# The last four steps of a decoder-layer kernel: first-layer chunks of batch 14 among the last transposed scores, and the last batch's second layer, norm and store by halves of the tokens

## What is computed

```python
x = _layernorm(x + _L0_attn_ref(x, w_qkv, w_proj, q_norm_w, k_norm_w))
x = _layernorm(x + _L0_xattn_ref(x, ctx, ctx, mask, Wq, Wk, Wv, Wo))
x = _layernorm(x + _L0_ffn_ref(x, ...))      # light_out + heavy_out
# feedforward: h = rmsnorm(x, gamma); h = gelu(h @ w1.T + b1); h @ w2.T + b2
```

## Time and profile before

| | us |
|---|---|
| median of 3 runs | 975.88 (974.96 to 978.18) |
| profiled execution, its own time | 978.16 |
| its span, first to last instruction | 976.40 |
| PE busy over the span | 888.3 (91%) |
| DVE busy | 725.3 (74%) |
| POOL busy | 537.9 (55%) |
| ACT busy | 496.8 (51%) |
| mean granted PE clock | 0.960 of 2.4 GHz |

### The profile page before, as it was taken

How to read it: one execution, slowest core, us unless ns; L and a number is a source line. 1 busy time by engine, 2 the same in 40 slices (tenths; PEclk the granted TensorE clock), 3 DMA queues, 4 the chain that set the end, 5 groups by cost and what they waited for, 6 DMA issues and landing times. The chain is left out here.

```text
span 976.4 us, 21698 instructions
## 1 busy us (share of the span) xinstructions
PE 888.3 (91%) x7712; PEld 689.7 (71%) x7712; DVE 725.3 (74%) x1764; ACT 496.8 (51%) x1063; POOL 537.9 (55%) x1047
## 2 busy tenths in 40 slices
PE   3367897999999999999999999999999999999886
PEld 2335565787868787777878787877778686767576
DVE  7788687878788878879787888788887877663411
ACT  1132444646475655656464756556464746455332
POOL 7554465646564756656565647657565656162421
PEclk9669898999999999999999999999999999999888
DMA  3794383727476654818275666738283656613000
GB/s 110 120 173 68 52 110 50 106 33 109 51 100 78 98 78 65 111 37 110 34 119 59 100 78 80 97 54 107 44 109 42 95 72 88 77 31 49 14 11 21
DMA packets 79644, 74.22 MB, mean 76 GB/s; under 512 B 8593, under 2 KB 78897, under 8 KB 79537
## 3 DMA queue, kind: packets, MB, share of 16 engines
q1 hardware_dynamic: 75008, 68.11, 50.5%
q10 hardware_dynamic: 4528, 4.73, 1.9%
HBM read 17.49 MB, written 4.20 MB: 22 GB/s over the span
## 5 line engine op out<-in xcount | busy, mean ns | idle before, releaser
L768 ACT ACTIVATE pr<-bank 128x384 f32<-128x384 f32 x512 | 240.0, 500 | 188.1 <-PE bank L370 187.0
L946 DVE TENSOR_REDUCE mx<-bank 128x3 f32<-128x384 f32 x512 | 266.4, 552 | 89.7 <-PE bank L370 87.5
L1311 POOL TENSOR_SCALAR_AFFINE_SELECT pr<-pr 128x256 f32<-128x256 f32 x512 | 222.1, 448 | 132.3 <-ACT pr L768 130.1
L370 PE MATMUL bank<-w,g 128*128 128x256 f32 x576 | 170.8, 389 | 1.1 <-ACT g L780 1.1
L370 PE MATMUL bank<-cmaskb,idb 128*128 128x256 bf16 x512 | 143.3, 280 | 27.7 <-DMA stk2k<-nat1k 13.7
L780 ACT ACTIVATE g<-bank,b 128x256 f32<-128x256 f32 x144 | 67.8, 473 | 83.5 <-PE bank L370 83.2
L1335 POOL TENSOR_TENSOR xTlow<-xT,xThigh 128x512 fp32r<-128x512 f32 x16 | 20.8, 1301 | 149.8 <-ACT xThigh L702 149.8
L370 PEld LDWEIGHTS bank<-w,g 128*128 128x128 f32 x576 | 89.6, 190 | 5.2 <-ACT g L780 1.5
L370 PEld LDWEIGHTS bank<-cmaskb,idb 128*128 128x128 bf16 x512 | 50.1, 98 | 50.5 <-DVE mx L946 22.5
L370 PE MATMUL bank<-stk2k,stk2q 97*128 97x128 bf16 (+1 forms) x512 | 85.1, 253 | 0.0
L370 PE MATMUL bank<-stk1q,stk1k 100*128 100x256 bf16 (+1 forms) x512 | 80.1, 254 | 2.4 <-DMA stk1q<-mT 1.0
(11 more groups left out here) (166 smaller groups left out, 1832.5 us busy)
## 6 DMA issues: line engine op xcount, KB each, us to landing
stk1q<-nat1q SPq DMA_DIRECT2D x90, 128.0 KB, 4.5
stk1k<-nat1k SPq DMA_DIRECT2D x90, 128.0 KB, 5.4
stk2k<-nat2k SPq DMA_DIRECT2D x90, 128.0 KB, 4.6
stk2q<-nat2q SPq DMA_DIRECT2D x90, 128.0 KB, 5.7
xT<-in_xT SPq DMA_DIRECT2D x16, 256.0 KB, 5.9
ctxT<-in_ctxT SPq DMA_DIRECT2D x16, 256.0 KB, 6.0
x<-in_x SPq DMA_DIRECT2D x16, 256.0 KB, 5.7
out_x<-x SPq DMA_DIRECT2D x16, 256.0 KB, 2.2
```

Source lines behind the costliest of these rows:

```text
L370: return nc.tensor.matmul(out, lhsT, rhs, start=start, stop=stop, skip_group_check=check)
L768: nc.scalar.activation(pr[:, h % (2 * HG), :], ring_bank("T", a, b, h)[:, 0:3 * P], ACT.Exp, scale=HD ** -0.5)\
L946: V.tensor_reduce(mx3[:, h, :], scored[:, 0:3 * P].rearrange("p (k t) -> p k t", k=3), AX.X, ALU.max, negate=True).then_inc(s_mx[a], 1)
L1311: G.affine_select(out=slot, in_=slot, compare_op=ALU.is_ge, fill=0.0, base=0, pattern=[[0, 2], [1, P]], channel_multiplier=-1).then_inc(s_ ...
```

## The change

Only steps 15 to 19 differ.

- Step 15: the second half of batch 12's second layer (`FFN1`) moves from phase 3 to phase 4 (`FFN1_LATE`). Its residual and statistics on DVE move behind the norm of batch 15, its inverse deviation on POOL behind the last mask. The inverse deviation of batch 15 moves from head 13 to head 10.
- Step 16: four chunks of batch 13 stay in phase 1, five move to between the cross scores of phase 2; its first half's second layer moves to later heads. ACT loads GELU's table with a one-element GELU ahead of the step's work. Eight chunks of batch 14 move from step 17 to phase 4 of step 16, among the transposed cross scores of batch 15; each has half a bank of its own (banks 5, 6, 7, 4), so none waits for a GELU.
- Step 17: only chunk 8 of batch 14 stays. The eight other GELUs run on ACT after the last exponential; the copy for batch 15's output projection stands after seven of them (`COPY2_LAST`). The cross output of batch 15 uses banks 0, 1, 2 and 0. The transposes of its normalised tokens move from behind head 12 to head 3 of phase 3, so that they stand behind 12 of the 18 second-layer products of batch 14. The exponential's table is not loaded any more.
- Step 18: `last_ffn` runs the last batch's first layer in four banks, with the second layer of the first token half four chunks behind it, then the second half. Each half has a bank, a residual, statistics, inverse deviation, norm (on DVE) and store of its own.

```diff
+        def token_bank(b, t):
+            return bank[t if b == B - 1 else TOK_BANK[t]]
...
+        def hidden_out(b, j):
+
+            if b == B - 2 and j < LIGHT:
+                return bank[(5, 6, 7, 4)[j // 2]][:, j % 2 * T:(j % 2 + 1) * T]
+            if b == B - 2:
+                return bank[OT_BANK][:, T:2 * T]
+            return bank[(1, 2, 5, 6)[j % 4] if b == B - 1 else HIDDEN_BANK[j % 2]][:, 0:T]
...
-                if live(i - 4):
+                if i - 4 == B - 1:
+                    for t in range(TT):
+                        sp.wait_ge(s_x[3], TT * (B - 1) + t + 1)
+                        load(io["out"][B - 1, t * P:(t + 1) * P, :], xo[3][:, t, :], s_out)
+                elif live(i - 4):
...
                 if live(b + 1):
                     pe.wait_ge(s_mT[2], b + 2)
+                else:
+                    pe.wait_ge(s_g, FCH * (B - 2) + 6)
                 four_transposes(XNT_BANK, xn).then_inc(s_xnt, 1)
...
-                if j == 0:
+                if b == B - 1:
+                    if j == 0:
+                        pe.wait_ge(s_xnT, B)
+                        pe.wait_ge(s_on[2], TT * B)
+                    elif j == 1:
+                        pe.wait_ge(s_onT[2], B)
+                    elif j < 4:
+                        pe.wait_ge(s_g, FCH * (B - 2) + 2 * j - 2)
+                    else:
+                        pe.wait_ge(s_g, FCH * b + j - 3)
+                elif b == B - 2:
+                    if j == 0:
+                        pe.wait_ge(s_xnT, b + 1)
+                        pe.wait_ge(s_va[2], B)
+                    elif j == 2:
+                        pe.wait_ge(s_rest[2], 2 * B)
+                    elif j == 4:
+                        pe.wait_ge(s_mT[2], B)
+                    elif j == 6:
+                        pe.wait_ge(s_y[3], b)
+                    elif j == LIGHT:
+                        pe.wait_ge(s_oT[2], NG * B)
+                elif j == 0:
...
+            def last_ffn_out(t, j):
+
+                b = B - 1
+                pe.wait_ge(s_g, FCH * b + j + 1)
+                if t == 1 and j == 0:
+                    pe.wait_ge(s_y[2], B)
+                last = mm(bank[(3, 0)[t]][:, 0:D], g[:, j, t * P:(t + 1) * P], w2[:, j, :], j == 0, j == FCH - 1)
+                if j == FCH - 1:
+                    last.then_inc(s_o[3], 1)
+
+            def last_ffn():
+
+                for j in range(FCH + 4):
+                    if j >= 4:
+                        last_ffn_out(0, j - 4)
+                    if j < FCH:
+                        hidden(B - 1, j)
+                for j in range(FCH):
+                    last_ffn_out(1, j)
...
+                if l == B - 1:
+                    return last_ffn()
...
-                if live(l):
-                    for j in range(FCH):
+                if l == B - 2:
+                    add(6, hidden, l, LIGHT)
+                elif live(l):
+                    for j in range(FCH if l < B - 3 else HIDDEN_AHEAD):
                         add(HIDDEN_AT[j], hidden, l, j)
...
+                if l == B - 3:
+                    for j in range(HIDDEN_AHEAD, FCH):
+                        add(HIDDEN_BEHIND[j - HIDDEN_AHEAD], hidden, l, j)
                 if live(l):
                     for j in range(FCH):
-                        add(FFN0_AT[j], ffn_out, l, 0, j)
+                        add((FFN0_LATE if l == B - 3 else FFN0_AT)[j], ffn_out, l, 0, j)
...
-                    add(XNT_AT, transpose_xn, f)
-                if live(l):
+                    add(XNT_LAST if f == B - 1 else XNT_AT, transpose_xn, f)
+                if live(l) and l != B - 4:
...
+                if l == B - 4:
+                    for j in range(FCH):
+                        add(FFN1_LATE[j], ffn_out, l, 1, j)
+                if f == B - 2:
+                    for j in range(LIGHT):
+                        add(HIDDEN_LATE[j], hidden, f, j)
...
+                if c == B - 1:
+                    nc.scalar.activation(warmg[:, :], minus_half[:, 0:1], ACT.Gelu)
                 if live(c):
                     high_part(2, c, 0, 1)
                 for j in range(FCH):
-                    if j == COPY2_AT and live(f):
+                    if j == (COPY2_LAST if f == B - 1 else COPY2_AT) and live(f):
                         copy_out(f)
-                    if j == MIDQ_AT and live(c):
+                    if j == (0 if c == B - 1 else MIDQ_AT) and live(c):
                         mid_part(2, c, 0, 1)
...
-                wait(act, s_warm, i + 2)
-                nc.scalar.activation(warm[:, :], minus_half[:, 0:1], ACT.Exp).then_inc(s_warm, 1)
+                if i <= B:
+                    wait(act, s_warm, i + 2)
+                    nc.scalar.activation(warm[:, :], minus_half[:, 0:1], ACT.Exp).then_inc(s_warm, 1)
...
+            def last_tokens(t):
...
+                V.tensor_tensor(y[3][:, t, :], bank[(3, 0)[t]][:, 0:D], x2b[:, t, :], ALU.add).then_inc(s_ylast, 1)
...
+                V.bn_stats(st[3][:, t, :], y[3][:, t, :]).then_inc(s_bn[3], 1)
...
+                V.bn_aggr(mv[3][:, t, :], st[3][:, t, :]).then_inc(s_mv[3], 1)
+                dve.wait_ge(s_rslast, t + 1)
...
+                V.tensor_scalar(xo[3][:, t, :], y[3][:, t, :], mv[3][:, t, 0:1], rstd[3][:, t:t + 1],
+                                ALU.subtract, ALU.mult).then_inc(s_x[3], 1)
...
+                if l == B - 1:
+                    last_tokens(0)
+                    last_tokens(1)
+                elif live(l) and l != B - 4:
+                    residual_ffn()
...
                 if live(s):
                     layer_norm(1, s)
+                if l == B - 4:
+                    residual_ffn()
...
+                if l == B - 1:
+                    last_deviation(0)
+                    last_deviation(1)
                 roots = {}
-                if live(l):
+                if live(l) and l != B - 4 and l != B - 1:
                     roots[RSTD3_AT] = lambda: inverse_deviation(3, l)
                 if live(s):
-                    roots[RSTD1_AT] = lambda: inverse_deviation(1, s)
+                    roots[RSTD1_LAST if s == B - 1 else RSTD1_AT] = lambda: inverse_deviation(1, s)
...
+                if l == B - 4:
+                    inverse_deviation(3, l)
...
-MAX2_AT, XNT_AT = 5, 12
+MAX2_AT, XNT_AT, XNT_LAST = 5, 12, 3
+HIDDEN_AHEAD, HIDDEN_BEHIND = 4, (1, 2, 4, 5, 7)
+FFN0_LATE = (8, 9, 10, 11, 12, 13, 14, 15, 16)
+FFN1_LATE = (2, 4, 5, 6, 8, 10, 11, 12, 14)
+HIDDEN_LATE = (3, 4, 5, 6, 8, 9, 10, 12)
+COPY2_LAST = 7
...
-RSTD3_AT, RSTD1_AT = 3, 13
+RSTD3_AT, RSTD1_AT, RSTD1_LAST = 3, 13, 10
```

More of the change, by code:

```diff
@@ L250, in values_of, with dim_bank, proj_bank @@
             return va1[b % 2] if a == 1 else va2
+        def token_bank(b, t):
+            return bank[t if b == B - 1 else TOK_BANK[t]]
+        def dim_bank(b):
+            return bank[2 if b == B - 1 else DIM_BANK]
+        def proj_bank(a, b):
+            return bank[0 if a == 2 and b == B - 1 else PROJ_BANK[a]]
+        def hidden_out(b, j):
[4 more added lines that the diff above has]
+            return bank[(1, 2, 5, 6)[j % 4] if b == B - 1 else HIDDEN_BANK[j % 2]][:, 0:T]
         h2 = HD // 2
@@ L475, in hidden @@
                 elif j == 1:
[L476 to L479, removed]
+                    pe.wait_ge(s_oT[2], NG * (b + 2))
                 else:
                     pe.wait_ge(s_g, FCH * b + j - 1)
-                out = bank[HIDDEN_BANK[j % 2]][:, 0:T]
+                out = hidden_out(b, j)
                 products = [(w, x, c) for w, x in ((w1h, xnh), (w1h, xnl), (w1l, xnh)) for c in range(C)]
@@ L572, in out_tokens @@
                 for t in range(TT):
-                    if t == 0:
+                    if b == B - 1:
+                        pe.wait_ge(s_exp[2], H * B)
+                    elif t == 0:
                         if live(b + 3):
                             pe.wait_ge(s_va[1], b + 4)
-                        elif live(b + 1):
+                        else:
                             pe.wait_ge(s_rest[2], 2 * (b + 1) + 1)
-                        else:
-                            wait(pe, s_onT[2], b)
                     else:
@@ L585, in out_tokens @@
                     for gr in range(NG):
-                        last = nc.tensor.transpose(bank[TOK_BANK[t]][:, gr * P:(gr + 1) * P],
+                        last = nc.tensor.transpose(token_bank(b, t)[:, gr * P:(gr + 1) * P],
                                                    oT[:, gr, t * P:(t + 1) * P], idf[:, :])
@@ L605, in out_proj @@
                 for t in range(TT):
-                    last = tok_proj(bank[PROJ_BANK[a]][:, t * D:(t + 1) * D], onT[a], t, (None, wo1, wo2)[a], 0, D)
+                    last = tok_proj(proj_bank(a, b)[:, t * D:(t + 1) * D], onT[a], t, (None, wo1, wo2)[a], 0, D)
                 last.then_inc(s_o[a], 1)
@@ L711, in copy_dims @@
             def copy_dims(dst, k):
```

(9 more changed lines are left out.)

36 lines of the change are left out of this document (21 added, 15 removed).

## The result

The changed kernel takes 967.86 us (median of 4 runs, 966.26 to 968.68); the kernel before, run beside it on the same chip, 977.03 (974.96 to 982.03). The ratio on record is 0.9897, with a 95% interval of 0.9855 to 0.9938: some 1% faster (the ratio of the two medians is 0.9906). The profiled execution of the changed kernel took 968.68, its span 966.9; that of before 978.16 and 976.40. So the profiled pair shows 9.5 us of gain where the sum had 11.4.

The account below looks back on a forecast made before the run. The tail was taken as PE work with holes, the clock falling behind some of them. Seven stage terms sum to -11.4 us, giving 964.5 from the median 975.88 (966.8 from the profiled execution); range 960 to 970.5, own 962 to 967.

Parts of the forecast that it names:

- Stage 3: Rest of the step up to batch 15's cross scores, 888.19 to 916.59: change 0 us, between -1.6 and +1.6.
- Stage 1: Transposed self-attention scores of batch 15, 861.00 to 871.19: loses nine second-layer products; 8.9 us, 1.3 less.
- Rival A: Clock falls again: Stage 1 at 11.98 us (+3.1) or Stage 4 starting at half clock (+2.7); total 967.5; chance 0.18.
- Stage 2: Batch 14's transposed cross scores and next step's start, to 888.19: moved products fill waits, clock kept; 15.5 us, 1.5 less.
- rival F: Step 15's reordering does nothing, Stage 1 and Stage 2 as before, ruled by the self-attention chain; total 967.3; chance 0.11.
- Stage 4: Transposed cross scores of batch 15, 916.59 to 931.15: takes in eight chunks at full clock; 14.3 us, 0.25 less.
- E: Slower: the clock that fell in Stage 4 does not come back, Stage 5's second layer slowed too; 984.7; chance 0.04.
- Stage 5: Both layers of batch 14, 931.15 to 953.03: keeps one chunk of nine, projection 3.5; 16.65 us against 21.88, 5.2 less.
- Rival B: Clock stays up through the hole in Stage 5, the last output projection takes 1.9 us; total 962.8; chance 0.08.
- Rival C: The GELU table switch in Stage 5 costs its drain of 1.38 us; total 965.9; chance 0.04.
- Stage 6: Both layers of batch 15, 953.03 to 970.16: loses the GELU wait and slow start; 15.0 us, 2.1 less.
- Stage 7: What follows the last matmul: run on 128 tokens instead of 256; 5.2 us against 6.24, 1.05 less.

Follow-up runs that it names:

- ahead6: Changed kernel with six first-layer chunks of batch 13, not four, ahead of batch 15's cross scores and three between them: 968.10 us, ratio 0.9906.
- ahead8: Changed kernel with eight first-layer chunks of batch 13, not four, ahead of batch 15's cross scores and one between them: 965.82 us, ratio 0.9879.
- before2: The kernel before the change, unaltered, profiled once more: 974.57 us in its one run.
- chunks_back: Changed kernel with batch 14's nine first-layer chunks back in the last cross step, two alternating banks, last projection's copy behind four GELUs: 972.02 us, 0.9964.
- serial: Changed kernel with the last step not interleaved: nine chunks, then the second layer of each token half in turn: 968.30 us, ratio 0.9930.
- tuned_fill: Changed kernel, eight batch 13 chunks ahead, transposes moved in Stage 3, batch 14 chunks in late waits, earlier GELU table, projection copy behind six GELUs: 961.65 us, 0.9844.

## Why the prediction came out as it did

964.5 was forecast, 967.86 measured, inside 960.0 to 970.5 and just outside the forecast's own 962 to 967. Of the 3.4 us between, the stages explain 1.9 (968.68 against the 966.8 worked out for a profiled execution); the rest is that the profiled execution of before lay 2.3 above its median and that of after only 0.8. The stages up to the fourth came out 3.2 longer than the sum had them, the last three 1.1 shorter; the range, which reaches 6 us above the forecast, takes that in, although stage 3 left its own bound. Of the signs that the prediction named for its being wrong, two appeared: a granted clock of 0.50 in stage 1 (from 865 to 867 us) and scores of batch 15 that wait for their queries (1.80).

- **Stage 3** is the step that failed: "I take 0, between -1.6 and +1.6"; it was +2.25, beyond my bound. The two causes were named (the copy ahead of the output projection, 0.69; the stacked queries' DMA, 1.80), but the second got no price of its own. A price by the last byte would still have been short: PE starts 1.2 us after it, and without that part the wait is 0.6. ahead6 shows that the start is fixed by the transfer, and with ahead8 that giving the chunks back takes the loss down to 0.56 and then away.
- **Stage 1**: 8.9 forecast, 9.37 measured with a fallen clock, 8.37 when it stays. Rival A's event occurred, at a third of its price (1.0, not 3.1): of what its row, the second bare stage, took above the first, the clock can have been only a part; the rest wasn't taken apart. That 967.86 lies next to A's 967.5 is no merit of A; stage 3 made the difference.
- **Stage 2**: 15.5 forecast, 15.90. The products took the holes at no cost, the projection ran in 1.95 at full clock, the new wait for the last mask is 0.61 (0.65 forecast). What rival F had and the sum had not: a chain off PE sets most of the length (16.17 in before2), so that little was to be had here but the clock.
- **Stage 4**: 14.3 forecast, 14.35, clock 1.00, the wait for the last mask 1.05 as in the earlier trace rows (1.2 in the sum). The filling and the clock are confirmed by chunks_back; D and E fall. That the size fits to 0.05 is luck: PE's work is 12.82 where the sum had 12.1, its waits 1.53 where the sum had 2.15. The 0.55 for the first chunk did not come: the low half of its tokens is ready at 917.44, and the chunk starts at 917.50, straight behind the scores.
- **Stage 5**: 16.65 forecast, 16.40. Projection at 4.5 after the copy (4.6 forecast), 3.68 long (3.5 forecast), transposes without a wait. Rival B, the clock that stays up, occurs too, in four profiles of seven, and is worth 1.7. Neither branch was wrong; a single forecast for it was.
- **Rival C** falls: the table load starts 0.02 after the copy ahead of it and its GELU 0.01 after it, as in the earlier trace rows. On the Trainium skill's drain of 1.38 us ("ScalarE: Activation LUTs", "What ACT_TABLE_LOAD costs") the rows disagree a second time.
- **Stage 6**: 15.0 forecast, 14.55. Right in sign, wrong in cause: serial shows that the interleaving isn't needed, and that the wait for each product's own GELU is enough to remove the 0.56. And the term of 0.775 a chunk was read in two banks that alternate, where chunks start 0.82 and 0.73 apart by turns (957.49, 958.31, 959.04); in four banks it is 0.72 (chunks begin at 948.44, 949.16 and 949.88), so 6.5 + 8.05 = 14.55.
- **Stage 7**: 5.2 forecast, 4.80. From the last matmul to the end of the norm it is 0.97 shorter (1.05 forecast, though with the deviation at its old cost); from there to the end of the span it is 2.12 for 2.59. The store was left at its cost, but its last issue now carries 128 KB instead of 256. No run undoes the halves, so this rests on the rows alone.
- **Readings of the kernel before.** The prediction sees one fall of the clock, at 919.4, that ends between 956 and 957. By single microseconds there are two: the first ends between 932 and 933 (mean 0.60 there, 1.00 from 933 on), the second begins between 953 and 954 (0.64). The 0.96 of stage 5 in the earlier trace rows says the same. The argument against E, that chunks brought the clock back in some 3 us, is read off the second; in the first it stayed at 0.50 from 920 to 932, though PE was busy without a gap from 921 to 928. And ACT and POOL are not busiest in stage 4: by the earlier trace rows they are at 7.54 and 7.07 of 10.19 us in stage 1 and at 9.94 and 10.79 of 17.00 in stage 2. No term of the sum hangs on either.

## What to carry to other kernels

Before you take work out from in front of a transfer's first user, take the transfer's price from its first issue to the start of the instruction that waited for it, in a place where that wait is seen; the last byte on the DMA line is not the landing. Work that is moved into a stage set by another engine's chain is free up to the size of the holes, and here it kept the clock besides; once the holes are small (stage 4 of tuned_fill), the chain holds PE up: one chunk taken out of the stage and one moved into its last wait, 1.45 us of PE's work, gave 0.72. And profile a kernel whose clock falls somewhere more than once before you put a price on the fall.

## What the runs showed of the hardware

- Two stretches with short waits had two lengths in executions with the same instructions: 8.37 or 9.2 to 9.4 us (clock 1.00 or 0.82; five profiles each) and 14.7 or 16.0 to 16.3 (1.00 or 0.89 to 0.90; four profiles and three), and nothing between.
- Six transfers of 128 KB each, issued back to back by SP, move their last byte 7.0 to 7.2 us after the first issue (changed kernel, one execution); PE, where it waits for them, starts 8.38 to 8.43 after it, in eight executions.
- The time ahead of stage 1 varied by 3.6 us over the eleven profiles of the changed kernel and its variants, with the same instructions; the lengths of the stages behind repeat within 0.05 but for the clock.
